# A GRU over 512 steps: x's parts of R and H for two pairs of steps as seven block products in place of eight, with biases in the activations

## The reference

```python
Xz = x @ Wxz.T + bxz; Xr = x @ Wxr.T + bxr; Xh = x @ Wxh.T + bxh   # all steps
for each step:
    Z = sigmoid(xz + H @ Whz.T + bhz)
    R = sigmoid(xr + H @ Whr.T + bhr)
    H_tilda = tanh(xh + R * H @ Whh.T + bhh)
    H = Z * H + (1 - Z) * H_tilda
    Y = H @ Whq.T + bhq
out = x + Y
```

## Time and profile before

| | before |
|---|---|
| median of 3 runs | 2266.95 us (2266.01 to 2267.04) |
| profiled execution | 2266.79 us |
| its span | 2264.9 us |
| TensorE busy | 2248.5 us, 99% |
| VectorE busy | 1348.7 us, 60% |
| ScalarE busy | 817.2 us, 36% |
| GpSimd busy | 0.8 us |
| mean granted clock of TensorE | 0.997 |

### The profile page before, as it was taken

How to read it: one execution, slowest core, us unless ns; L and a number is a source line. 1 busy time by engine, 2 the same in 40 slices (tenths; PEclk the granted TensorE clock), 3 DMA queues, 4 the chain that set the end, 5 groups by cost and what they waited for, 6 DMA issues and landing times.

```text
span 2264.9 us, 183797 instructions
## 1 busy us (share of the span) xinstructions
PE 2248.5 (99%) x81984; PEld 2242.7 (99%) x81984; DVE 1348.7 (60%) x8961; ACT 817.2 (36%) x4610; POOL 0.8 (0%) x6
## 2 busy tenths in 40 slices
PE   7999999999999999999999999999999999999999
PEld 7999999999999999999999999999999999999998
DVE  3666666565666566666665656666666666666655
ACT  2333333333333333333333333333333333333333
POOL 0000000000000000000000000000000000000000
PEclk8999999999999999999999999999999999999999
DMA  4000000000000000000000000000000000000000
GB/s 155 21 24 21 24 21 24 21 24 21 23 22 23 22 22 23 22 23 22 23 22 23 22 23 22 23 21 24 21 24 21 24 21 24 21 24 21 24 21 22
DMA packets 112530, 58.48 MB, mean 26 GB/s; under 512 B 13056, under 2 KB 111488, under 8 KB 111616
## 3 DMA queue, kind: packets, MB, share of 16 engines
q1 hardware_dynamic: 112512, 58.21, 8.8%
HBM read 41.39 MB, written 16.78 MB: 26 GB/s over the span
## 4 chain that ended last, share of the span: by engine, by line
PE 98%; DMA 1%; SPq 0%; DVE 0%; issue 0%; ACT 0%; DVEq 0%
PE pre L191 59%; PE pre L161 30%; PE y_bank L171 10%; DMA xt<-in_x_t 1%; SPq L131 0%; SPq L133 0%; SPq L139 0%; DVE pre_t L286 0%; DVE reset_state L305 0%; DVE fresh L316 0%; SPq L137 0%; ACT z_not L265 0%; ACT cand L269 0%; DVE kept L310 0%; ACT r_gate L262 0%
## 5 line engine op out<-in xcount | busy, mean ns | idle before, releaser
L191 PE MATMUL pre<-wh,states 128*16 128x128 f32 x32768 | 991.2, 273 | 3.0 <-DMA wh<-in_w_hr 2.2
L286 DVE STREAM_TRANSPOSE pre_t<-pre 128x32 f32<-128x32 f32 (+2 forms) x3584 | 619.0, 217 | 609.5 <-PE pre L191 569.0
L191 PEld LDWEIGHTS pre<-wh,states 128*16 128x16 f32 x32768 | 902.6, 104 | 5.3 <-DMA wh<-in_w_hr 2.4
L161 PE MATMUL pre<-wx,xt 128*32 128x128 f32 x24576 | 859.8, 273 | 8.1 <-DMA xt<-in_x_t 3.3
L161 PEld LDWEIGHTS pre<-wx,xt 128*32 128x32 f32 x24576 | 692.4, 110 | 9.7 <-DMA xt<-in_x_t 3.8
L262 ACT ACTIVATE r_gate<-pre_t 128x16 f32<-128x16 f32 (+1 forms) x1536 | 234.6, 215 | 863.5 <-DVE pre_t L286 863.5
L191 PE MATMUL pre<-wh,reset_state 128*16 128x128 f32 (+1 forms) x16384 | 542.1, 273 | 0.0
L191 PEld LDWEIGHTS pre<-wh,reset_state 128*16 128x16 f32 (+1 forms) x16384 | 454.9, 104 | 0.7 <-DVE reset_state L305 0.4
L269 ACT ACTIVATE cand<-pre_t 128x16 f32<-128x16 f32 (+1 forms) x1536 | 235.1, 215 | 305.9 <-DVE pre_t L286 305.9
L171 PE MATMUL y_bank<-wq,states 128*32 128x128 f32 x8192 | 270.5, 273 | 1.5 <-DVE states L320 1.5
L310 DVE TENSOR_TENSOR kept<-z_gate,states 128x64 f32<-128x64 f32 x512 | 115.7, 226 | 239.6 <-ACT z_gate L266 239.6
(11 more groups left out here) (11 smaller groups left out, 10.5 us busy)
## 6 DMA issues: line engine op xcount, KB each, us to landing
xt<-in_x_t SPq DMA_DIRECT2D x256, 64.0 KB, 1.8
y_io<-in_x_res SPq DMA_DIRECT2D x256, 64.0 KB, 1.8
out<-y_io SPq DMA_DIRECT2D x256, 64.0 KB, 1.6
wx<-in_w_xr SPq DMA_DIRECT2D x1, 1024.0 KB, 5.9
wx<-in_w_xz SPq DMA_DIRECT2D x1, 1024.0 KB, 6.3
wx<-in_w_xh SPq DMA_DIRECT2D x1, 1024.0 KB, 8.4
wh<-in_w_hr SPq DMA_DIRECT2D x1, 1024.0 KB, 10.5
wh<-in_w_hz SPq DMA_DIRECT2D x1, 1024.0 KB, 12.3
```

Source lines behind the costliest of these rows:

```text
L161: mm = nc.tensor.matmul(pre[par][Q * j:Q * (j + 1), g, 0:P], xt[:, par, m, :], wx[g][:, m, P * j:P * (j + 1)], start=False, stop=(m == G - 1),
L191: mm = nc.tensor.matmul(pre[par][Q * j:Q * j + rows, g, 0:P], of, wh[g][:, m, P * j:P * (j + 1)], start=False, stop=(m == G - 1), skip_gro ...
L286: nc.vector.transpose(flat(pre_t[g][:, a:b]), pre[par][:, g, Q * a:Q * b]).then_inc(done, 1)
```

## The change

**Products.** With a pair's x split into halves of the input channels (0: blocks 0 and 1, 1: blocks 2 and 3), and A, B the turn's two pairs, x's parts of R and H are RA = A0 R0 + A1 R1, HA = A0 H0 + A1 H1, and the same for B: eight half products of 8 matmuls each, 64 a turn. After the change they are seven (Strassen's scheme in Winograd's form), 56 a turn: p1 = A0 R0, p2 = A1 R1, p3 = s4 H1, p4 = B1 t4, p5 = s1 t1, p6 = s2 t2, p7 = s3 t3. The sums t1 to t4 of the weights are made once (VectorE, t3 on GpSimd), the sums s1 to s4 of x each turn on GpSimd. p1 and p6 go to a bank `p16_bank`, p5 and p7 to banks of their own; RA is p1 + p2, HA is p1 + p6 + p5 + p3, RB is p1 + p6 + p7 + p4 and HB is p1 + p6 + p7 + p5. ScalarE and VectorE copy and add them into the gates' banks (`put_ra`, `copy_p16`, `put_rb` on ScalarE; `put_ha`, `put_hb` on VectorE). Z's part stays as it was (`project_z`).

**Banks.** R and H of a pair share a bank (`rh_bank`), Z has its own (`z_bank`), and y has one bank in place of two.

**Biases.** R's and H's are given to sigmoid and tanh as one value per partition, which differs by block, so each gate takes four activations of 16 columns. Z's bias is written to its bank as before.

**Order.** `add_y` stands between Z's transpose and `kept`; the three renewals are interleaved with `fresh`. x is loaded once a turn for both pairs (`xr`), and its second pair once more (`x_b`). The weights are loaded in another order, and the biases in two transfers in place of eight.

The core of the diff (declarations of tiles and semaphores, and the layout of the inputs, are left out):

```diff
+            def sums(n, first=False):
+                x_a0, x_a1, x_b0, x_b1 = xr[:, 0, 0:half], xr[:, 0, half:G], xr[:, 1, 0:half], xr[:, 1, half:G]
+                pool.wait_ge(xr_loaded, 16 * (n + 1))
+                nc.gpsimd.tensor_tensor(x_sum[1][:], x_b0, x_b1, ALU.add).then_inc(s1_ready, 1)
+                pool.wait_ge(s1_ready, n + 1)
+                nc.gpsimd.tensor_tensor(x_sum[2][:], x_sum[1][:], x_a0, ALU.subtract).then_inc(s2_ready, 1)
+                pool.wait_ge(s2_ready, n + 1)
+                nc.gpsimd.tensor_tensor(x_sum[4][:], x_a1, x_sum[2][:], ALU.subtract).then_inc(s4_ready, 1)
+                if not first:
+                    pool.wait_ge(p7_done, n)
+                nc.gpsimd.tensor_tensor(x_sum[3][:], x_a0, x_b0, ALU.subtract).then_inc(s3_ready, 1)
...
+            def product(to, of, w, first=0, end=half, start=False):
+                for m in range(first, end):
+                    for j in range(G):
+                        mm = nc.tensor.matmul(to[Q * j:Q * (j + 1)], of[:, m, :], w[:, m, P * j:P * (j + 1)],
+                                              start=start and m == 0, stop=(m == half - 1), skip_group_check=True)
+                return mm
...
+            def p1():
+                product(p16_bank[:, 0:P], xr[:, 0, 0:half], wx[R][:, 0:half], start=True).then_inc(p1_done, 1)
+            def p6(first, end):
+                product(p16_bank[:, 0:P], x_sum[2], w_sum[1], first, end)
+            def p5():
+                product(p5_bank[:, 0:P], x_sum[1], w_sum[0], start=True).then_inc(p56_done, 1)
+            def p7():
+                product(p7_bank[:, 0:P], x_sum[3], w_sum[2], start=True).then_inc(p7_done, 1)
+            def p2():
+                product(gate_bank(R, 0), xr[:, 0, half:G], wx[R][:, half:G])
+            def p3():
+                product(gate_bank(H, 0), x_sum[4], wx[H][:, half:G]).then_inc(xr_used, 1)
+            def p4():
+                product(gate_bank(R, 1), x_b[:, half:G], w_sum[3]).then_inc(xb_used, 1)
...
+                recur(R, i, 0, first)
+                recur(Z, i, 0, first)
+                pe.wait_ge(z_filled, 2 * i + 2)
+                pe.wait_ge(xb_loaded, 16 * (i + 1))
+                project_z(1, 0, 1)
+                recur(H, i, 0, first)
+                if first:
+                    pe.wait_ge(t_ready[2], 1)
+                pe.wait_ge(s3_ready, i + 1)
+                p7()
+                if not first:
+                    project_y(2 * i - 1, 1)
+                recur(R, i, 1)
+                recur(Z, i, 1)
+                project_z(1, 1, 2)
+                recur(H, i, 1)
+                project_z(1, 2, G)
+                if first:
+                    pe.wait_ge(t_ready[3], 1)
+                pe.wait_ge(rb_put, i + 1)
+                p4()
+                if not last:
+                    pe.wait_ge(xr_loaded, 16 * (i + 2))
+                    p1()
+                recur(R, i, 2)
+                recur(Z, i, 2)
+                if not last:
+                    pe.wait_ge(s2_ready, i + 2)
+                    pe.wait_ge(ra_put, i + 2)
+                    p6(0, 1)
+                recur(H, i, 2)
+                if not last:
+                    p6(1, half)
+                    p5()
+                if first:
+                    pe.wait_ge(wq_loaded, 2 * 16)
+                project_y(2 * i, 0)
+                recur(R, i, 3)
+                recur(Z, i, 3)
+                if not last:
+                    pe.wait_ge(z_filled, 2 * i + 3)
+                    project_z(0, 0, 1)
+                recur(H, i, 3)
+                if not last:
+                    project_z(0, 1, G)
+                    p2()
+                    pe.wait_ge(s4_ready, i + 2)
+                    pe.wait_ge(ha_put, i + 2)
...
+                    p3()
...
+            def put_ra(n):
+                act.wait_ge(p1_done, n + 1)
+                nc.scalar.copy(gate_bank(R, 0), p16_bank[:, 0:P]).then_inc(ra_put, 1)
+            def copy_p16(n):
+                act.wait_ge(p56_done, n + 1)
+                nc.scalar.copy(p16[:], p16_bank[:, 0:P]).then_inc(p16_copied, 1)
+            def put_rb(n):
+                act.wait_ge(hb_put, n + 1)
+                nc.scalar.copy(gate_bank(R, 1), p167[:]).then_inc(rb_put, 1)
...
+                    if c == 1:
+                        put_rb(i)
+                    elif c == 2 and not last:
+                        put_ra(i + 1)
+                    elif c == 3 and not last:
+                        copy_p16(i + 1)
+                    for m in range(G):
+                        act.wait_ge(r_turned[part_of(m)], t + 1)
+                        nc.scalar.activation(r_gate[:, m], pre_t[R][:, m, mine], ACT.Sigmoid,
+                                             bias=bias_rh[:, 0, m:m + 1]).then_inc(r_ready, 1)
...
+                        nc.scalar.activation(cand[:, m], pre_t[H][:, m, mine], ACT.Tanh,
+                                             bias=bias_rh[:, 1, m:m + 1]).then_inc(cand_ready, 1)
...
+            def put_ha(n):
+                dve.wait_ge(p16_copied, n + 1)
+                nc.vector.tensor_tensor(gate_bank(H, 0), p16[:], p5_bank[:, 0:P], ALU.add).then_inc(ha_put, 1)
+            def put_hb(n):
+                dve.wait_ge(p7_done, n + 1)
+                nc.vector.tensor_tensor(p167[:], p16[:], p7_bank[:, 0:P], ALU.add).then_inc(p167_ready, 1)
+                dve.wait_ge(p167_ready, n + 1)
+                nc.vector.tensor_tensor(gate_bank(H, 1), p167[:], p5_bank[:, 0:P], ALU.add).then_inc(hb_put, 1)
...
+                    if c == 1:
+                        put_hb(i)
+                    elif c == 3 and not last:
+                        put_ha(i + 1)
...
+                    if s == 1 and not (first and par == 0):
+                        add_y(2 * i + par - 1, 1 - par, i + par)
...
+                    take_fresh(t, 0)
+                    take_fresh(t, 1)
+                    renew(t, 0, new)
+                    take_fresh(t, 2)
+                    renew(t, 1, new)
+                    renew(t, 2, new)
...
+            load_xr(0)
             sp.dma_start(wx[R][:], w_x[R]).then_inc(wx_loaded[R], 16)
+            sp.dma_start(wx[H][:], w_x[H]).then_inc(wx_loaded[H], 16)
+            sp.dma_start(wh[R][:], w_h[R]).then_inc(wh_loaded[R], 16)
+            sp.dma_start(bias_in[:], b_rh).then_inc(bias_loaded, 16)
+            sp.dma_start(bias_z_in[:], b_z).then_inc(bias_loaded, 16)
             sp.dma_start(wx[Z][:], w_x[Z]).then_inc(wx_loaded[Z], 16)
             sp.wait_ge(zeroed, 2)
             sp.dma_start(states[:, 1, :, 2 * B:3 * B], h0).then_inc(h0_loaded, 16)
+            sp.dma_start(wh[Z][:], w_h[Z]).then_inc(wh_loaded[Z], 16)
+            sp.dma_start(wh[H][:], w_h[H]).then_inc(wh_loaded[H], 16)
             sp.dma_start(wq[:], w_q).then_inc(wq_loaded, 16)
+            sp.dma_start(bias_out[:], b_out).then_inc(wq_loaded, 16)
+            load_xb(0)
```

More of the change, by code:

```diff
@@ L19, with part_of, gru @@
 N = len(PARTS)
-def gru(nc, x_t, x_res, h0, w_x, w_h, w_q, b_gate, b_out, out):
-    pairs = x_t.shape[0]
-    turns = pairs // 2
+def part_of(m):
+    return next(h for h, (a, b) in enumerate(PARTS) if a <= m < b)
+def gru(nc, x_t, x_res, h0, w_x, w_h, w_q, b_rh, b_z, b_out, out):
+    turns = x_t.shape[0]
+    pairs = 2 * turns
+    half = G // 2
     with ExitStack() as ctx:
@@ L100, in pair_loop, with load_xr @@
             with eng.Fori(1, turns - 1) as i:
[L101 to L104, removed]
+                turn(i, first=False, last=False)
+            turn(turns - 1, first=False, last=True)
         @block.sync
         def _(sp):
-            def load_xt(k, par):
-                sp.dma_start(xt[:, par], x_t[k]).then_inc(xt_loaded[par], 16)
+            def load_xr(n):
+                sp.dma_start(xr[:], x_t[n]).then_inc(xr_loaded, 16)
@@ L111, in load_res, with load_xb, turn @@
+            def load_xb(n):
+                sp.dma_start(x_b[:], x_t[n][:, 1]).then_inc(xb_loaded, 16)
             def load_res(k, par):
                 sp.dma_start(y_io[:, par], x_res[k]).then_inc(y_loaded[par], 16)
-            def pair(i, par, first, last):
-                k = 2 * i + par
+            def turn(i, first, last):
                 if not last:
[L118 to L125, removed]
@@ L127, in _ @@
-            load_xt(0, 0)
-            sp.dma_start(wx[R][:], w_x[R]).then_inc(wx_loaded[R], 16)
[L129 to L133, removed]
+                    sp.wait_ge(xr_used, i + 1)
@@ new lines, in turn @@
+                    sp.wait_ge(s3_ready, i + 1)
+                    load_xr(i + 1)
+                for par in range(2):
+                    k = 2 * i + par
+                    if par == 1 and not last:
+                        sp.wait_ge(xb_used, i + 1)
+                        load_xb(i + 1)
+                    if not (first and par == 0):
+                        sp.wait_ge(y_added, k)
```

(26 more changed lines are left out.)

261 lines of the change are left out of this document (139 added, 122 removed).

## The result

The changed kernel takes **2423.7 us** (2421.9 to 2424.2 in 4 runs) against 2266.9 us before: the ratio is 1.069, with a 95% interval of 1.068 to 1.070. It is 157 us slower. The forecast was 2505 us; the range of its main case was 2400 to 2585, so the measured time lies near its lower end.

The account below looks back on a forecast made before the run. TensorE bound before, the chain over four engines after: second step at 27.7, 511 steps of 4.80 = 2452.8, end about 3, extras 19; span 2503, so 2505 us. Main case's range 2400 to 2585; overall range 2232 to 2585, about 0.8 inside.

Parts of the forecast that it names:

- its main case: Bias operand makes every step chain-bound: 2505 us, range 2400 to 2585 (top: operand price 0.115 without extras), chance 0.58.
- What bounds the kernel, and how near the chain is: Steady loop: TensorE bound at 4.37 us a step; cover behind R used up, behind H to 0.1 us.
- The operand's price: R's and H's activations on ScalarE: b = 0.092 us added to each one's duration and distance, between 0 and 0.115.
- read beside the activation in front: Rival on ScalarE: operand adds latency only, distance stays 0.115; period 4.25 us, 2236 us, faster; chance 0.14.
- the free operand: Rival on ScalarE: the bias operand costs nothing, 56 us and the start's 1.5 go, 2209 us, faster; chance 0.16.
- 4.06 + 8b: Chain of one step over the engines, in us, b being the operand's price: 4.80 at b = 0.092.
- The price at which the gain is lost, b = 0.04: Operand price in us at which the step's chain lengthens enough to lose the 56 us saved in matmuls.
- Other work on VectorE and ScalarE: Moved sums and copies: put_hb before R's transposes in step 1 costs 0.05 us a turn, the rest nothing.
- The other items put at nothing: add_y between Z's transpose and kept, y's single bank, put_ra, copy_p16 and the fills: no cost.
- a rival with a chance of 0.06 at its full size: GpSimd's sums hold VectorE's products: 0.6 us a turn, 2568 us, over 2600 with b near its top; chance 0.06.
- The start: Loads before the second step: less issue brings it 0 to 3 us earlier, 1.5 taken, less 0.4 for a longer first step.
- TensorE busy under 92%: Sign for the forecast in the steady loop, with waits for reset_state and states and a step of 4.8 us.

Follow-up runs that it names:

- the fastest kernel: Changed kernel's seven products, but R's and H's biases filled into PSUM, three activations a gate without operand, GpSimd's sums started later: 2209.2 us, ratio 0.975 to the kernel before.
- the 16.5 us above: Seven products with biases by PSUM, sums not moved, VectorE back in its old order (three fresh, then three renewals): 2236.9 us against 2220.4 interleaved.
- The two placements of the sums: GpSimd's four sums as in the changed kernel, 2423.7 us, or the same kernel with them started after the state of step 1 is ready, 2408.0 us.
- both kernels with three a gate: Kernel before with a bias operand of zeros, 2334.4 us; changed kernel with three activations a gate in place of four, each with the bias operand, 2264.7 us.

## Why the prediction was right, and where it was off

**What bounds the kernel, and how near the chain is:** right. The kernel before loses nothing to a fourth activation and 68 us to 0.09 us a read, so its cover was used up nearly as far as the earlier trace rows show. The fourth activation delays only the last part, which TensorE wants later than the first; the operand delays every part.

**The operand's price:** right in kind and nearly in size. Taken: 0.092 us in duration and distance, by the part of an activation that the next one overlaps. Measured: 0.089 (296 less 207) and 0.086 (201 less 115). The reason given, one trip to memory and back for each, is not shown: the price was set equal to an overlap that the earlier trace rows show, and no run here tells a common cause from chance, so that it came out within 6 ns is in part luck. The rival "read beside the activation in front" would have left the distance at 0.115; it fell, as did the free operand. The Trainium skill gives about 93 ns for a pointer operand ("ScalarE: Activation LUTs", section "What ACT_TABLE_LOAD costs"). The measured 89 agrees within 4 ns. It also gives an overlap of about 93 ns for neighbours, and here that held with the operand too (296 less 201 is 95).

**The period:** 4.06 + 8b, with b for the price of the operand, had one term wrong. From kept to H's transposes the forecast took 0.22 us from the last step, as if VectorE set it. It is 0.14 in the changed kernel (1002.43 to 1002.57). In the earlier trace rows H's own matmuls ended at the same moment. Their weight loads began 0.73 us after R's transposes, and 1.15 for 16 matmuls gives 2259.93, so that row did not show VectorE's pace:

```profile
2258.78 0.81 PEld L191 LDWEIGHTS pre<-wh,reset_state 128*32 128x32 f32 x32 [0.19 <-DVE reset_state L305]
```

That is 0.08 x 511 = 41 us. The smaller price of the operand, 6 ns in each of six distances and 3 ns in two durations, is 0.04 us a step, another 21. The last 0.04 of the 0.16 us between 4.80 and the measured 4.64 is spread over the other gaps, none more than 0.03 off: some 20 us, which completes the 81 between 2505 and 2424 to within the rounding. All of these erred the same way. The top of the range is also 5 us high by its own terms: 0.023 x 8 x 511 more and 19 of extras less is 2580.

**The price at which the gain is lost, b = 0.04:** with 3.98 in place of 4.06 it is about 0.05. No run has that price.

**Other work on VectorE and ScalarE:** put_hb was to cost 0.05 us a turn. It costs nothing: VectorE is idle for 0.32 us before R's transposes in step 1, the step shown above. The forecast had the sums end at U + 2.16 (U is the start of H's transposes), with the operand in the chain ahead of them, but the transposes possible at U + 2.10, which is 1.17 + 0.93 without it. With 4b they come at 2.47, and 0.31 us is left. The other items put at nothing show no cost. The interleaved renewals were said to nearly pay for the narrower cover; in the fastest kernel, where GpSimd's sums do not hold VectorE, they leave nothing to pay, and beside the sums they are worth the 16.5 us above.

**GpSimd:** the mechanism was put down as a rival with a chance of 0.06 at its full size, and in the sum with 0.1 us a turn. Measured: 0.12 (15 us over 127 turns). A sum takes 0.32 us and four of them 1.4 with their waits, where 0.25 and 1 were taken. By the Trainium skill ("SBUF — State Buffer", section "Who interferes with whom") a VectorE instruction contends with a GpSimd one that reads SBUF if it has two inputs in SBUF, and not with at most one outside some fast modes. The two placements of the sums agree. That one shuts the other out for a whole instruction they do not show: kept, started together with a sum of 0.32 us, was 0.16 longer, and started 0.19 behind one it was not held.

**The start:** the second step's weights come 2.3 us earlier (26.52 in the changed kernel, against 28.79 in the earlier trace rows), the longer first step included, where 1.1 was forecast. TensorE had x_b at 24.06, where the second pair's x came at 25.29: 1.2 us. The rest is the clock, which the forecast left out. Both kernels wait for x just before, 3.3 us before the change and 2.5 after. The mean granted clock was 0.50 (the lower level, 1.2 GHz) between 20 and 26 us and 0.69 in the next six before the change, and 1.00 (2.4 GHz) in both stretches after. The 32 weight loads of H in the first step took 1.66 us before and 0.91 after. Before the change TensorE had also waited for weights from 14 us on (2.2 and 0.6 us); after, it worked from 14.70 to 20.5 us without a break. Whether that is the reason no run tests.

**What was to show it:** "TensorE busy under 92%" was wrong as a sign, though the loss was there: the page says 98%. The count of matmuls in a stretch is the right sign.

## What to carry to other kernels

Where engines hand a small tile round in a loop, an operand like this bias is paid once for each instruction in a row on the chain, so count the reads in series before adding one: here eight a step turned a gain of 45 us (the same kernel without the operand) into a loss of 157. A constant can often enter where an idle engine prepares it, in this case in the accumulator ahead of the matmuls. And judge a nearly saturated TensorE by matmuls per microsecond and by its weight loads, not by its busy share.

## What the runs showed of the hardware

- An activation of 16 columns lasts 207 ns without and 296 ns with a per-partition bias operand, and the next one starts 115 or 201 ns after it. A column of zeros costs the same as real biases (300 ns in both kernels with three a gate).
- A GpSimd sum of two 128x64 fp32 tiles takes 0.32 us. Beside it a VectorE product of two SBUF tiles takes up to 0.16 us more (kept 0.39 for 0.23), by where the two fall; a VectorE sum with one operand in PSUM takes 0.29 us as it does alone.
- Copies by ScalarE and sums by VectorE into banks that TensorE then adds onto cost TensorE no time that these runs show: 36648 matmul records in 1000 us in the fastest kernel, 36649 in the kernel before.
